# Feed-forward stage 3 of a gated transformer chain: four stacked copies of the low-rank rows, high and low weights in one tile, and the low-rank output accumulated in the last hidden tile's bank

## What is computed

```python
def _L2_ffn_ref(x, gate_w, up_w, down_w, gate_a, gate_b, up_a, up_b, down_a, down_b):
    D_MODEL = 512
    D_HIDDEN = 1376
    RANK = 16
    def _matmul_lora(x, w, a, b, scale=1.0):
        out = jnp.einsum('bsd,hd->bsh', x, w)
        out = out + jnp.einsum('bsr,hr->bsh', jnp.einsum('bsd,rd->bsr', x, a), b) * scale
        return out
    gate = _matmul_lora(x, gate_w, gate_a, gate_b)
    up = _matmul_lora(x, up_w, up_a, up_b)
    hidden = jax.nn.silu(gate) * up
    out = _matmul_lora(hidden, down_w, down_a, down_b)
    return out
...
x = x + jnp.tanh(g_ffn[2]) * _L2_ffn_ref(_layernorm(x, axis=-1), L2_ffn_gate_w, L2_ffn_up_w, L2_ffn_down_w, L2_ffn_gate_a, L2_ffn_gate_b, L2_ffn_up_a, L2_ffn_up_b, L2_ffn_down_a, L2_ffn_down_b)
x = x + jnp.tanh(g_xattn[3]) * _L3_xattn_ref(_layernorm(x, axis=-1), ctx_4096, L3_xattn_Wq, L3_xattn_Wk, L3_xattn_Wv, L3_xattn_Wo)
```

## Time and profile before

| | us |
|---|---|
| median of 3 runs | 3003.39 (3002.08 to 3007.03) |
| the profiled execution | 2998.09 |
| span from its first to its last instruction | 2996.1 |
| PE busy in the span | 2846.4 (95%) |
| DVE busy | 1788.6 (60%) |
| ACT busy | 1094.7 (37%) |
| POOL busy | 898.2 (30%) |

### The profile page before, as it was taken

How to read it: one execution, slowest core, us unless ns; L and a number is a source line. 1 busy time by engine, 2 the same in 40 slices (tenths; PEclk the granted TensorE clock), 3 DMA queues, 4 the chain that set the end, 5 groups by cost and what they waited for, 6 DMA issues and landing times.

```text
span 2996.1 us, 47997 instructions
## 1 busy us (share of the span) xinstructions
PE 2846.4 (95%) x14914; PEld 2368.0 (79%) x14914; DVE 1788.6 (60%) x4181; ACT 1094.7 (37%) x3288; POOL 898.2 (30%) x780
## 2 busy tenths in 40 slices
PE   7997799999999999888999999989999999999998
PEld 5665588888888888667888888878877888888887
DVE  5666754465455446675777777744452555555557
ACT  4564233333333333123444444421113444444442
POOL 5433144243334324232222222235432222222210
PEclk9999999999999999999999999999999999999999
DMA  3000011011111111011000011111111000001000
GB/s 130 15 4 19 20 46 43 25 56 35 39 39 46 37 30 50 22 47 29 29 29 29 29 32 32 29 36 53 50 46 46 25 29 26 25 27 29 25 8 29
DMA packets 55235, 104.40 MB, mean 35 GB/s; under 512 B 6672, under 2 KB 6928, under 8 KB 54928
## 3 DMA queue, kind: packets, MB, share of 16 engines
q1 hardware_dynamic: 51840, 94.39, 10.8%
q10 hardware_dynamic: 3216, 7.81, 0.7%
HBM read 100.09 MB, written 2.10 MB: 34 GB/s over the span
## 4 chain that ended last, share of the span: by engine, by line
PE 85%; DVE 9%; ACT 3%; issue 3%; ACTq 0%; DVEq 0%
PE proj L578 38%; PE outp L578 22%; PE score L578 12%; PE value L578 9%; PE turned L807 4%; ACT probs L1232 2%; DVE top L1589 1%; DVE stats L1383 1%; DVE xt_lo L1412 1%; DVE x L1530 0%; DVE probs L1597 0%; DVE nt L1355 0%; PE turned L625 0%; DVE vz L1479 0%; DVE probs L1407 0%
## 5 line engine op out<-in xcount | busy, mean ns | idle before, releaser
L527 POOL TENSOR_TENSOR w_hi<-raw,zero 128x512 fp32r<-128x512 f32 x352 | 377.3, 1072 | 1793.3 <-PE proj L578 633.9
L1530 DVE SCALAR_TENSOR_TENSOR x<-outp,g_inv,x 128x512 f32<-128x512 f32 x768 | 556.4, 748 | 380.9 <-PE outp L578 379.9
L531 POOL TENSOR_TENSOR w_lo<-raw,w_hi 128x512 fp32r<-128x512 f32 x352 | 455.5, 1294 | 27.6
L578 PE MATMUL proj<-xt_hi,w_lo 128*128 128x512 f32 x928 | 394.6, 425 | 9.3 <-DVE xt_lo L1412 4.8
L578 PE MATMUL proj<-xt_hi,w_hi 128*128 128x512 f32 x928 | 368.4, 397 | 0.0
L578 PE MATMUL proj<-xt_lo,w_hi 128*128 128x512 f32 x928 | 366.1, 395 | 0.0
L578 PE MATMUL outp<-w_hi,a_lo 128*128 128x512 f32 x800 | 330.7, 413 | 30.5 <-DVE a_lo L1649 22.7
L578 PE MATMUL outp<-w_hi,a_hi 128*128 128x512 f32 x800 | 315.6, 394 | 0.0
L578 PE MATMUL outp<-w_lo,a_hi 128*128 128x512 f32 x800 | 314.8, 394 | 0.0
L1102 ACT ACTIVATE pT<-turned 128x512 f32<-128x512 f32 x320 | 192.0, 600 | 288.3 <-PE turned L807 288.3
L1232 ACT ACTIVATE probs<-probs,top 128x128 f32<-128x128 f32 x512 | 199.6, 391 | 238.6 <-DVE top L1573 126.8
(11 more groups left out here) (245 smaller groups left out, 5080.7 us busy)
## 6 DMA issues: line engine op xcount, KB each, us to landing
raw<-in_stream SPq DMA_DIRECT2D x352, 256.0 KB, 2.6
ctx_raw<-in_ctx_t ACTq DMA_DIRECT2D x4, 512.0 KB, 6.0
x<-in_x_in ACTq DMA_DIRECT2D x2, 1024.0 KB, 12.1
pb<-in_position_bias ACTq DMA_DIRECT2D x1, 2048.0 KB, 9.3
out<-x SPq DMA_DIRECT2D x8, 256.0 KB, 2.0
qw<-in_qweight ACTq DMA_DIRECT2D x1, 768.0 KB, 3.9
ln_w<-in_ln_weight ACTq DMA_DIRECT2D x1, 256.0 KB, 2.8
q_bi<-in_q_bias ACTq DMA_DIRECT2D x1, 256.0 KB, 2.6
```

The costliest lines, as they stand in the source:

```text
L527: pool.tensor_tensor(w_hi[:, k, :], raw[:, k % RAW, :], zero[:, :].to_broadcast([P, D]), ALU.add)\
L531: pool.tensor_tensor(w_lo[:, k, :], raw[:, k % RAW, :], f32(w_hi[:, k, :]), ALU.subtract)\
L578: m = pe.matmul(out_, l, r, start=start, stop=stop, skip_group_check=True)
L1530: dve.scalar_tensor_tensor(out=x[:, b, :], in0=O[no_f(k) % 2][:, :], scalar=scale, in1=x[:, b, :], op0=ALU.mult, op1=ALU.add)\
```

## The change

It works on F2 alone.

- Chunk A: before anything else in `swiglu()`, ACT waits for the chunk and copies columns 0 to 63 of each group of 128 to columns 64 to 127, in `w_hi` and in `w_lo` (two instructions). The low-rank rows then stand four times in the result, in partitions 0, 32, 64 and 96. DVE makes the remainder in two of them (32 and 96; two instructions per half in place of one).
- Chunk `("l", j)`: ACT copies the low part of gate_b and up_b into partitions 64 to 127 of the `w_hi` tile, and arranges down_a's low and high parts in further columns of `w_hi` (three instructions, `lora_rows(j)`). `lora_rows(0)` stands before the first silu, `lora_rows(j + 1)` before the second silu of tile j. PE waits for each by the new semaphore `lora`.
- `gate_or_up`: one low-rank matmul in place of two, and it comes last in the accumulation, not first. 13 matmuls in place of 14.
- `down_low`: two matmuls per half in place of three.
- The end: `lora_rows(11)` (two copies) puts the high and low parts of down_b in one tile, and `down(10)` adds one matmul with it to each token tile's three, in the same bank. The 8 token tiles after it, 16 matmuls and 8 additions on DVE, are gone.

```diff
--- before.py
+++ after.py
@@ -444,7 +444,7 @@
         FS = [
             sems("_F0", "proj low l_turned probs s_exp sx s_turned hm h_hi h_lo outp x_acc tiny"),
             sems("_F1", "proj low l_turned probs s_exp sx s_turned hm h_hi h_lo outp x_acc tiny"),
-            sems("_F2", "proj low_hi low_lo silu hid h_hi h_lo dl dl_hi dl_lo outp x_acc"),
+            sems("_F2", "proj low_hi low_lo silu hid h_hi h_lo lora dl dl_hi dl_lo outp x_acc"),
             sems("_F3", "codes wn w_turned wT_hi wT_lo outp biased x_acc"),
         ]
 
@@ -459,7 +459,7 @@
         ADDS = []
         for n in range(4):
             ADDS.append((AS[n]["x_acc"], len(ATT[n].tile)))
-            ADDS.append((FS[n]["x_acc"], {0: B, 1: 2 * B, 2: (HIDDEN_TILES + 1) * B, 3: B}[n]))
+            ADDS.append((FS[n]["x_acc"], {0: B, 1: 2 * B, 2: HIDDEN_TILES * B, 3: B}[n]))
 
         def phase_start(eng, n):
 
@@ -995,46 +995,40 @@
                     else:
 
                         c = f_chunk(2, ("A",))
+                        pe.wait_ge(s["lora"], 1)
                         wait_norm(norm, (i + 1) * (B // 2))
                         by_feature(S[i][:, :], c, "x", i, last=True).then_inc(s["proj"], 1)
                         owed[0] += i
                 pe.wait_ge(AS[3]["j_out"], ATT[3].early)
-                def stacked(dst, weights, low, weights_stand, start, stop):
-
-
-                    for no, w in enumerate(weights):
-                        l, r = (w, low) if weights_stand else (low, w)
-                        m = mm(dst, l, r, start and no == 0, stop and no == 1)
-                        if not (stop and no == 1):
-                            told(m)
-                    return m
-
                 def gate_or_up(j, t, w):
 
                     no = 2 * j + t
-                    lora, c = f_chunk(2, ("l", j)), f_chunk(2, ("gu"[w], j))
+                    lora, c = CHUNK_AT[("F2", ("l", j))], f_chunk(2, ("gu"[w], j))
                     if w == 0 and no >= 2:
                         pe.wait_ge(s["hid"], no - 1)
+                    dst = (J if t == 0 else S)[w][:, :]
+                    for kt in range(KT):
+                        mm3(dst, ring(c, tokens(kt)), acts("x", kt, half(t)), kt == 0, False)
                     if j == 0:
                         pe.wait_ge(s["low_lo"], t + 1)
-                    dst = (J if t == 0 else S)[w][:, :]
-                    stacked(dst, ring(lora, tokens(w)), M2["low"][:, half(t)], True, True, False)
-                    for kt in range(KT):
-                        last = kt == KT - 1
-                        m = mm3(dst, ring(c, tokens(kt)), acts("x", kt, half(t)), False, last, last)
-                    m.then_inc(s["proj"], 1)
+                    pe.wait_ge(s["lora"], j + 2)
+                    mm(dst, w_hi[:, lora % RING, tokens(w)], M2["low"][:, half(t)], False, True)\
+                        .then_inc(s["proj"], 1)
                     owed[0] += t
 
                 def down_low(j):
 
-                    lora, last = f_chunk(2, ("l", j)), j == HIDDEN_TILES - 1
+                    lora, last = CHUNK_AT[("F2", ("l", j))], j == HIDDEN_TILES - 1
+                    w = w_hi[:, lora % RING, tokens(2)]
                     for t in range(2):
                         pe.wait_ge(s["h_hi"], 2 * j + t + 1)
+                        told(mm(TV[t][:, :], w, M2["h_hi"][:, j % 2, half(t)], j == 0, False))
                         pe.wait_ge(s["h_lo"], 2 * j + t + 1)
-                        h = M2["h_hi"][:, j % 2, half(t)], M2["h_lo"][:, j % 2, half(t)]
-                        m = mm3(TV[t][:, :], ring(lora, tokens(2)), h, j == 0, last, last)
+                        m = mm(TV[t][:, :], w, M2["h_lo"][:, j % 2, half(t)], False, last)
                         if last:
                             m.then_inc(s["dl"], 1)
+                        else:
+                            told(m)
                         owed[0] += t
 
                 def down(j, tiles):
@@ -1045,7 +1039,13 @@
                         if no > 2:
                             pe.wait_ge(s["x_acc"], no - 2)
                         h = M2["h_hi"][:, j % 2, tokens(b)], M2["h_lo"][:, j % 2, tokens(b)]
-                        mm3(O[b % 2][:, :], h, ring(d), True, True, last=True).then_inc(s["outp"], 1)
+                        if j < HIDDEN_TILES - 1:
+                            mm3(O[b % 2][:, :], h, ring(d), True, True, last=True).then_inc(s["outp"], 1)
+                            continue
+                        mm3(O[b % 2][:, :], h, ring(d), True, False)
+                        pe.wait_ge(s["dl_lo"], b // 4 + 1)
+                        mm(O[b % 2][:, :], M2["dl"][:, tokens(b)], w_hi[:, CHUNK_AT[("F2", ("b",))] % RING, :],
+                           False, True).then_inc(s["outp"], 1)
                     if B - 1 in tiles:
                         owed[0] += 1
 
@@ -1058,13 +1058,8 @@
                         if j:
                             down(j - 1, range(2 * no, 2 * no + 2))
                 down_low(HIDDEN_TILES - 1)
+                pe.wait_ge(s["lora"], HIDDEN_TILES + 2)
                 down(HIDDEN_TILES - 1, range(B))
-                c = f_chunk(2, ("b",))
-                for b in range(B):
-                    pe.wait_ge(s["dl_lo"], b // 4 + 1)
-                    pe.wait_ge(s["x_acc"], HIDDEN_TILES * B + b - 1)
-                    stacked(O[b % 2][:, :], ring(c), M2["dl"][:, tokens(b)], False, True, True)\
-                        .then_inc(s["outp"], 1)
                 owed[0] += 1
 
             def quantised():
@@ -1290,6 +1285,12 @@
             def swiglu():
                 s, norm = FS[2], 5
                 phase_start(act, norm)
+                c = CHUNK_AT[("F2", ("A",))]
+                act.wait_ge(w_done, c + 1)
+                for w in (w_hi, w_lo):
+                    rows = w[:, c % RING, :].rearrange("p (k f) -> p k f", k=KT)
+                    o = copy(rows[:, :, 64:128], rows[:, :, 0:64])
+                o.then_inc(s["lora"], 1)
                 for kind, i in NORM_ORDER[2]:
                     if kind == "early":
                         early_out(3, i)
@@ -1298,8 +1299,25 @@
                     else:
                         act.wait_ge(s["proj"], i + 1)
                         copy(M2["low"][:, half(i)], S[i][:, :]).then_inc(s["low_hi"], 1)
+                def lora_rows(j):
+
+                    c = CHUNK_AT[("F2", ("l", j) if j < HIDDEN_TILES else ("b",))]
+                    act.wait_ge(w_done, c + 1)
+                    slot = c % RING
+                    if j == HIDDEN_TILES:
+                        copy(w_hi[64:96, slot, :], w_hi[0:32, slot, :])
+                        copy(w_hi[96:128, slot, :], w_lo[0:32, slot, :]).then_inc(s["lora"], 1)
+                        return
+                    copy(w_hi[64:128, slot, 0:2 * P], w_lo[0:64, slot, 0:2 * P])
+                    copy(w_hi[:, slot, 2 * P + 64:2 * P + 96], w_lo[:, slot, 2 * P:2 * P + 32])
+                    copy(w_hi[:, slot, 2 * P + 96:3 * P], w_hi[:, slot, 2 * P:2 * P + 32])\
+                        .then_inc(s["lora"], 1)
+
+                lora_rows(0)
                 for j in range(HIDDEN_TILES):
                     for t in range(2):
+                        if t:
+                            lora_rows(j + 1)
                         no = 2 * j + t
                         act.wait_ge(s["proj"], 2 + 2 * no + 1)
                         if no >= 2:
@@ -1820,13 +1838,14 @@
                 s, norm = FS[2], 5
                 g = gate[:, 6:7]
                 norm_all(norm)
-                def low_parts(what, banks, hi_done, lo_done):
+                def low_parts(what, banks, hi_done, lo_done, starts):
 
                     for t in range(2):
                         dve.wait_ge(s[hi_done], t + 1)
-                        rows = M2[what][32:64, half(t)]
-                        dve.tensor_tensor(rows, banks[t][32:64, :], f32(rows), ALU.subtract)\
-                            .then_inc(s[lo_done], 1)
+                        for r in starts:
+                            rows = M2[what][r:r + 32, half(t)]
+                            o = dve.tensor_tensor(rows, banks[t][r:r + 32, :], f32(rows), ALU.subtract)
+                        o.then_inc(s[lo_done], 1)
 
                 def hidden(j, t):
 
@@ -1846,7 +1865,7 @@
                     for b in tiles:
                         add_tile(s, g, j * B + b + 1, b)
 
-                low_parts("low", S, "low_hi", "low_lo")
+                low_parts("low", S, "low_hi", "low_lo", (32, 96))
                 for j in range(HIDDEN_TILES):
 
                     if j:
@@ -1857,9 +1876,8 @@
                     hidden(j, 1)
                     if j:
                         add_tiles(j - 1, range(6, B))
-                low_parts("dl", TV, "dl_hi", "dl_lo")
+                low_parts("dl", TV, "dl_hi", "dl_lo", (32,))
                 add_tiles(HIDDEN_TILES - 1, range(B))
-                add_tiles(HIDDEN_TILES, range(B))
 
```

## The result

The change takes 2984.42 us (median of 4 runs, 2984.00 to 2985.32) against 3004.99 for the kernel before (4 runs, 3002.08 to 3007.03): 20.6 us less, ratio 0.9933 with the 95% interval 0.9915 to 0.9950. Two later groups of runs, each with its own runs of the kernel before, gave 2980.26 against 3002.42 (0.9927, 0.9911 to 0.9944) and 2984.35 against 3003.65 (0.9938, 0.9922 to 0.9954): 22.2 and 19.3 us less. The forecast was 19.9 less.

What follows compares the result with a forecast made beforehand. PE alone was taken to bound the loop, PE and DVE handing tiles over to bound start and end. Terms of -14.7, -5.6 and +0.4 us sum to -19.9, from 3003.39 to 2983.5 us; range 2978 to 2989.

Steps and rivals of the forecast that it cites:

- Term 1: Loop over hidden tiles: 64 matmuls fewer at 0.230 us each, all on PE's path, -14.7 us.
- The page's rule on the gap: Loop's matmul spacing: the skill's 131 ns would make the loop's gain 8.4 us; the prediction used the measured 0.230 us.
- Term 2: End of the stage: pairs of token tiles in a 2.03 us cycle, last addition earlier, -5.6 us.
- Term 3: Start of the stage: ACT's two 256-column copies delay PE's next projection, +0.4 us.
- rival B: TensorE's clock in layer 4: one more slow stretch gives 2985.2 to 2986.9 us; chance 0.08.
- Rival A: End not shortened as laid out: cycle 2.5 us, waits in the loop, 2988.4 us in the middle; chance 0.10.
- C: No gain: a ring of waits between engines holds the loop's tile at 19.8 us, 3003 us; chance 0.03.
- D: Slower: ACT's copies become the loop, past 9.0 us of room each microsecond costs 11 us; chance 0.02.

Runs made afterwards that it cites:

- low_first: The change with the single low-rank matmul put first in each gate and up product instead of last: 2991.26 us.
- yardstick: The change once more, unedited, as the reference for the follow-up kernels: 2980.26 us.
- old_end: The change with the old end: low-rank output a round of its own, two matmuls and an addition per token tile: 2989.99 us.
- copies_later: The change with ACT's two copies of chunk A behind the first early output rows instead of ahead of them: 2979.58 us.

## Why the prediction was right, and where it was off

**Term 1, -14.7, measured -16.46.** Its mechanism holds: no wait in the loop, 20 matmuls of `down_low` at 0.233 each, ACT's copies within their room. The price was mis-sized. It was taken as constant, 0.230 us for each of the 910 starts; it fell to 0.228 for the 846 that stay, since the low-rank product moved to the tail (low_first puts it back and loses 2.33), and 846 x 0.002 is the missing 1.7 us. A tile takes 80 x 0.228 = 18.2 us, not 18.4. That the place costs anything was no part of the working. Of the upper bound of this term's loss, 44 waits by 0.10, nothing came: in the yardstick the start behind a fulfilled wait for `lora` comes 226.7 ns after the one ahead, as without a wait.

**The page's rule on the gap** (the Trainium skill, "TensorE: Matmul & The Clock Gate", section "Back-to-back issue gap", about 131 ns in a stream): no run of this kernel comes near it in this loop; the lowest mean distance in a position is 224 ns. Taking the row was right.

**Term 2, -5.6, measured -5.64**, by old_end too. The cycle of 2.03 is 2.04. The end is 14.11 us, 13.7 was put down beside 19.4, both from 0.35 us later.

**Term 3, +0.4, measured +0.56** (0.59 by copies_later). The two copies add 0.61 us to PE's idle time (2.08 - 1.47), and only 0.05 of it was hidden, against 0.26 reckoned. What wasn't seen is that this longer idle time can be followed by a low stretch, which adds 1.3 us.

**The sum, -19.9 for the median.** The terms' errors, -1.7 and +0.2, make -21.5 with the clock full. Measured medians are -19.3, -20.6 and -22.2. That the forecast of the first group came within a microsecond is in part luck: the terms were 1.6 us too small, and medians of the same two kernels differ by 2.9 from group to group, which hides it.

The profiled execution was forecast at 2978.2 us and took 2984.41, 6.2 more. Its trace has 88.7 us at the low level, that of the kernel before 71.7: 17 us or five stretches more. Two of them lie ahead of the stage, which begins 2.4 us later; one each in start and end, 1.30 and 1.36 us; one in layer 4, which is 3.0 us longer, 1.7 of them not explained. These 8.1 us take -21.5 to -13.4, the difference of the spans. So rival B's mechanism was at work in this execution, and more of it than its one stretch. It looked for it only in layer 4, where one of the five lies, and priced a stretch of 3.4 us at 1.7, while 1.3 to 1.4 were measured in start and end.

**The others.** Rival A fell, its cycle of 2.5 us was 2.04, and C as well. The load of 86% that A names is DVE's (16.66 of 19.40 us); PE's is 77% (15.02). D's room of 9.0 us measured 8.9, its price per microsecond was too low: 11 us were reckoned without the clock, which adds some 40% to what the waits cost (16 us to 38).

## What to carry to other kernels

Where one engine is busy without a gap, count what is taken from it and price it by the spacing of that stretch, then ask whether what remains keeps its spacing: here the order within a bank was worth 0.9% of the loop. At the end of a stage count the cycle of the handing over, not instructions. Sizes under 0.1% are to be read in parts of the trace whose clock is full; the median of a few runs doesn't show them.

## What the runs showed of the hardware that was not expected

**More low stretches at the start with more idle time.** In the executions profiled, those with 2.08 us of idle time on PE at the stage's start had a low stretch there in 6 of 9; those with 1.47 us in none of 5. If the idle time made no difference, such a split would come in about 3 of 100 cases (84 of 3003 ways to place the six), so this is likely but not shown. In the end a low stretch came in 4 of 11 for the new order and none of 3 for the old one, though PE idles 1.2 to 1.3 us there in both; the counts are too small to tell them apart.

**PE can stop a second time in layer 4.** All kernels show PE idle for some 3 us at two places 166 us apart, where it waits for nothing that the profile has ("issue"). Two of them, old_end and low_first, stop once more right behind. PE in low_first:

```profile
2465.66 1.12 PE L578 MATMUL score<-kT,qT 128*128 x4 [3.04 <-issue]
...
2469.12 0.90 PE L807 MATMUL turned<-ident,probs 128*128 128x128 f32 x3 [2.23 <-issue]
...
2633.68 1.59 PE L578 MATMUL score<-kT,qT 128*128 x4 [3.04 <-issue]
...
2637.94 0.90 PE L807 MATMUL turned<-ident,probs 128*128 128x128 f32 x3 [2.46 <-issue]
```

That is 4.69 us in low_first and 4.27 in old_end (1.86 and 2.41), in code that neither edit touches. What it makes of the time shows between two additions of DVE, the same in each kernel, one some 160 us ahead of the first place and one behind the second: first the yardstick, then low_first.

```profile
2301.70:2632.90 331.20, 324.06 (x1794) 278.52 (x1793) 183.28 (x385) 140.54 (x418) 74.18 (x64) 0.98 0.10 27
```

```profile
2305.90:2642.00 336.10, 324.10 (x1793) 278.06 (x1792) 183.38 (x384) 140.54 (x418) 74.23 (x64) 0.98 0.10 26
```

They differ by 4.9 us, and old_end's (335.40) by 4.2. Each of the two has 3.4 us more at the low level in it, some 1.3 us, so that the stops themselves cost about 3.6 and 2.9. Over the whole rest old_end is 3.2 us longer than the yardstick and low_first 5.3. That 5.64 and the stops' 4.27 come near the 9.7 us between the medians of old_end and the yardstick is thus in part chance, and low_first, 10.8 above the middle of the two others of its group, isn't fully accounted for by 1.75 + 2.33 and its stops.

The places are those of a loop: the trace has PE's compare-and-branch there, 3.66 and 3.56 us long in the yardstick and 3.36 in old_end. PE's two earlier loops (from 605 and 1472 us on in the yardstick) have the same instruction, 0.22 to 0.24 us long at each jump back. One thing that differs is the size of a pass: 1223 and about 970 records of PE in those loops, weight loads and waits included, 2109 in layer 4's. The Trainium skill, "Runtime: NRT & Kernel Launch", section "Instruction fetch mechanics", says that an engine's instructions are fetched ahead in blocks and strictly in order, and that a taken branch out of the blocks at hand has to wait for a fetch. The long branch in the long loop agrees with that. The second stop would fit a border between blocks close behind the branch's target, which moves with the number of instructions ahead; no run here shows where the borders lie, so this reading is open. What is shown is the price: two edits in one stage came with 3 to 5 us in another that they don't touch.
